# An edge-list graph kernel: GpSimd differences in the histogram, edge groups every 6.0 slots

## The chip, the cores and the metric

The kernel runs on one core of one Trainium2 chip. The metric is the device time of one execution in microseconds (us); lower is better. A profiled execution is traced instruction by instruction, and all rows below come from one such execution of the kernel before. Engines are named as in the profile: PE is TensorE's matmuls and PEld its weight loads, DVE is VectorE, ACT ScalarE, POOL GpSimd, SP SyncE, whose queue issues most plain transfers. A q behind a name (POOLq) is that engine's instruction queue.

## The reference

One graph layer over 6,250 nodes with 256 features and 200,000 edges (src, dst), sorted by dst:

```
out_deg = max(segment_sum(ones, src), 1);  in_cnt = segment_sum(ones, dst)
t1  = x @ W1
msg = (t1[src] + x[src] * x[dst] @ W2) / (sqrt(out_deg[src]) * sqrt(out_deg[dst]))
agg = segment_sum(msg, dst)
emb = leaky_relu(where(in_cnt > 0, t1 + agg, 0) + b, 0.01);  emb = emb / max(|emb|, 1e-12)
out = layernorm(x + emb)
```

Since the products with W1 and W2 are linear, the kernel sums scaled rows of x over the edges of a destination first, and multiplies by W1 and W2 once per block of 128 nodes.

## The kernel before

**Stage 1, the histogram of src.** It gives the out-degrees. A source number is split into a low part (7 bits) and a high part. The edges are cut into 98 groups of 16 tiles of 128 edges (`HT = 16`, one edge per partition and tile). For a group, VectorE makes the high hots (`hi_hot1`, L327: 16 x 50 columns, 1 where a ramp 0, 1, 2, ... equals the edge's high part) and, for a *plain* group, the low hots (`lo_hot1`, L336: 16 x 128 columns). Each of these is one tensor_tensor with is_equal, whose operands are the ramp (`iota_b`, in SBUF) and a pair-wise copy of the part (`hi2`, `lo2`). TensorE then does 16 matmuls of low by high hots, added up in `hist_ps` (L510).

For a *signed* group VectorE makes the high hots only. ScalarE makes steps in place of the low hots: 16 activations Sign of ramp + (0.5 - low), 128 columns each, with a bias per partition (`steps`, L445), which are -1 left of the edge's part and +1 from it on. They are added up in `step_ps` and turned into counts at the end by one matmul with a matrix of differences (`differ`, L536). Groups whose number modulo 11 is 3, 7 or 10 are signed: 26 of 98; 72 are plain.

Order and buffers: each engine goes through its own list of groups in order. VectorE may make the high hots of group g when group g - 4's matmuls are done (`HI_RING = 4`), the low hots of a plain group when those of the plain group two before are; the steps have two buffers as well. In between, VectorE does at group 8 the tables for the gathers (`gather_tables`) and at group 16 the keys of the edge lists (`list_keys`, L369 to L376); before groups 4 to 15 it waits for one gathered set of list rows each (`s_wrow`). TensorE turns the lists from group 17 on (`turn_lists`), and ScalarE copies them (`list_table`). GpSimd issues the 15 gathers of list rows, then four affine_selects (L273, L276), then waits for the end of the stage.

**Scaling.** With the degrees known, VectorE and ScalarE scale x and split it into three 16-bit parts (`yp`), and SP's queue stores them to `y_parts` in DRAM, in 8 chunks.

**Stage 2, the node blocks.** A loop over slots, written out by hand, gives every engine its order. 30 of the 49 node blocks are *dense*: their edges are counted into matrices (per slot, a window of 4 matmuls, L818, from hots that VectorE makes at L948 against a ramp in PSUM, `iota_w`) and multiplied with `yp` (L837, 9 or 12 matmuls per slot from slot 16 to 495). 19 blocks are *gathered*: 77 groups of 8 x 128 edges, whose rows GpSimd gathers from `y_parts` (L702, 8 indirect DMAs a group, 4 groups of buffers), and TensorE adds them up with hots (`group`, L799 and L805). VectorE adds a group's sums to `gT` and `cnt` three slots later (`accumulate`); TensorE's next group waits for that. Group g stands at slot `FIRST_SLOT + g * SLOTS_A_GROUP[0] // SLOTS_A_GROUP[1]`, 17 + 6.2 g, and is moved back where it would meet the sums of a gathered block. Each block has an end: its sums (gathered blocks: `turn_sums`, L853 and L854), transposes (`turn_uv`, L864), the weights (L876), then normalization on VectorE and ScalarE and the store of the block's output. The ends of dense blocks stand every 16 slots (the last at 496), those of gathered blocks halfway between where their last group is in (the last three at 472, 488 and 504).

At the start of the stage VectorE copies the ramp into PSUM, makes the first hots, and clears `gT`, `cnt` and sets `ones_f` (L1033 to L1035). GpSimd sets one column of ones (L707), then waits for the last store of `y_parts` and starts the gathers. After that a third stage, for graphs that do not fit these lists, is passed over.

Of the kernel before, what the change touches and what calls it, by code (L numbers as in the profile page):

```python
# [41 lines left out]
SLOTS_A_GROUP = (62, 10)  # L42
# [8 lines left out]
HI_RING = 4  # L51
SIGN_PERIOD = 11
SIGN_GROUPS = (3, 7, 10)
# [9 lines left out]
def build(nc, x, src, dst, w1, w2, bias, src_t, dst_t, starts, spans, out):  # L63
# [32 lines left out]
    with ctx:  # L96
# [9 lines left out]
        iota_h = sb("iota_h", [P, P], F16)  # L106
        w1_sb = sb("w1_sb", [P, H, D], F32)
# [24 lines left out]
        s_hist = sem("s_hist"); s_histall = sem("s_histall"); s_deg = sem("s_deg"); s_sqrt = sem("s_sqrt")  # L132
        s_hi = sem("s_hi"); s_r1 = sem("s_r1"); s_mid = sem("s_mid"); s_lo3 = sem("s_lo3")
# [8 lines left out]
        with ph1:  # L142
# [13 lines left out]
            lo_hot1 = sb1("lo_hot1", [P, 2, HT, P], BF16)  # L156
            hi_hot1 = sb1("hi_hot1", [P, HI_RING, HT, HI_COLS], BF16)
# [67 lines left out]
            kept_by = {b: next(i for i in range(2, len(signed)) if signed[i - 2] >= g) for g, b in turn_at.items()}  # L225

            with nc.Block() as block:  # L227
# [51 lines left out]

                @block.vector  # L280
                def _(dve):
# [31 lines left out]
                    nc.vector.tensor_copy(iota_b[:, :], iota_i[:, :])  # L313
# [6 lines left out]
                    def factor_hots(g):  # L320

                        part = sum(g * HT >= t1 for _, t1 in PAIR_PARTS)
                        dve.wait_ge(s_pairs1, 2 * (part + 1))
                        at = slice(g * HT, (g + 1) * HT)
                        if g >= HI_RING:
                            dve.wait_ge(s_hist, g - HI_RING + 1)
                        last = nc.vector.tensor_tensor(  # L327
                            hi_hot1[:, g % HI_RING, :, :].rearrange("p t (c two) -> p t c two", two=2),
                            iota_b[:, 0:HI_COLS].rearrange("p (c two) -> p c two", two=2).unsqueeze(1)
                            .to_broadcast([P, HT, HI_COLS // 2, 2]),  # L330
                            hi2[:, at, :].unsqueeze(2).to_broadcast([P, HT, HI_COLS // 2, 2]), ALU.is_equal)
                        if g in plain:
                            i = plain.index(g)
                            if i >= 2:
                                dve.wait_ge(s_hist, plain[i - 2] + 1)
                            last = nc.vector.tensor_tensor(  # L336
                                lo_hot1[:, i % 2, :, :].rearrange("p t (c two) -> p t c two", two=2),
                                iota_b[:, :].rearrange("p (c two) -> p c two", two=2).unsqueeze(1)
                                .to_broadcast([P, HT, P // 2, 2]),
                                lo2[:, at, :].unsqueeze(2).to_broadcast([P, HT, P // 2, 2]), ALU.is_equal)  # L340
                        last.then_inc(s_hot1, 1)
# [38 lines left out]
                    for g in range(HIST_GROUPS):  # L380
# [48 lines left out]
                def _(act):  # L429
# [11 lines left out]
                    def steps(i):  # L441
                        if i >= 2:
                            act.wait_ge(s_hist, signed[i - 2] + 1)
                        for t in range(HT):
                            last = nc.scalar.activation(lo_step[:, i % 2, t, :], iota_b[:, :], ACT.Sign,  # L445
                                                        bias=half_lo[:, signed[i] * HT + t:signed[i] * HT + t + 1])
                        last.then_inc(s_step, 1)
# [6 lines left out]
                    for i in range(len(signed)):  # L454
# [25 lines left out]
                def _(pe):  # L480
# [20 lines left out]
                    def histogram(g):  # L501
                        pe.wait_ge(s_hot1, g + 1)
                        if g in signed:
                            i = signed.index(g)
                            pe.wait_ge(s_step, i + 1)
                            into, low = step_ps, lo_step[:, i % 2, :, :]
# [34 lines left out]
        with ph2:  # L541
# [45 lines left out]
            iota_w = ps2("iota_w", [P, 512])  # L587
            iota_ps = iota_w[:, :].bitcast(F16)
# [4 lines left out]
            s_iotap = sem("s_iotap")  # L593
# [81 lines left out]
            with nc.Block() as block:  # L675
# [18 lines left out]
                def _(pool):  # L694
# [13 lines left out]
                    nc.gpsimd.drain().then_inc(s_ones, 1)  # L708
                    pool.wait_ge(s_ystore, 16 * len(X_CHUNKS))
# [73 lines left out]
                def _(pe):  # L783
# [116 lines left out]
                def _(dve):  # L900
# [164 lines left out]

        ph3 = ExitStack()
# [306 lines left out]
```

## Time and profile before

| | |
|---|---|
| median of 3 runs | 1077.23 us (1076.64 to 1593.53) |
| profiled execution | 1077.94 us, span of its instructions 1076.2 us |
| TensorE busy | 916.7 us (85%) in 13,011 matmuls |
| VectorE busy | 706.6 us (66%) |
| GpSimd busy | 610.5 us (57%), 586.8 of it the 616 gathers of L702 |
| ScalarE busy | 482.6 us (45%) |
| chain that ended last | TensorE 68%, VectorE 15%, issue 7%, GpSimd 6%, DMA 2% |

The shares are means over stages with different limits, so they are read together with the stretches of the stages: the histogram up to about 162 us, the scaling to 205, the start of the node blocks to about 223, the node blocks to about 1045 and their end. The chain of waits is followed back from the last instruction; what stands in it set the end at that place. In the groups of instructions, "idle before" is the idle time of the engine just before them, and behind the arrow stands what ended it.

### The profile page before, as it was taken

Reading aid. Unit: us, or ns where it says so; the run is one execution under the profiler, and the core shown is the slowest. Engines: PE = TensorE matmul, PEld = TensorE weight load, DVE = VectorE, ACT = ScalarE, POOL = GpSimd, SP = SyncE. Lnnn points to the kernel's source line nnn. Section 1 sums busy time; section 2 is a strip of 40 time slices with the busy share of each in tenths; the row PEclk is TensorE's granted clock in tenths of the full one; section 3 lists DMA queues with packets and bytes.
Section 4 is the critical chain, followed back from the end, with each engine's and each line's share of the span. In section 5 each row is a group of like instructions: output and inputs, shape, how many; then the busy total and the mean of one; then the engine's idle time right before and its main releaser. Section 6 shows DMA issues by size and latency. Waiting matters only on the chain.

```text
span 1076.2 us, 31326 instructions
## 1 busy us (share of the span) xinstructions
PE 916.7 (85%) x13011; PEld 813.4 (76%) x13011; DVE 706.6 (66%) x1524; ACT 482.6 (45%) x1357; POOL 610.5 (57%) x651
## 2 busy tenths in 40 slices
PE   3366660189999999999999999999999999999993
PEld 2255550078988888888988988988989888888882
DVE  8999998954566565665666566656656567466443
ACT  5799977343343343433434333433334334343311
POOL 4400000177777777777777775767767577777300
PEclk9985555589999999999999999999999999999995
DMA  9200003755566656566566655656646466566300
GB/s 314 67 2 2 2 2 135 253 158 161 168 170 177 179 168 179 167 177 178 170 172 176 175 167 144 177 148 176 178 145 178 136 177 180 157 173 170 94 20 21
DMA packets 68120, 155.83 MB, mean 145 GB/s; under 512 B 12006, under 2 KB 37668, under 8 KB 67972
## 3 DMA queue, kind: packets, MB, share of 16 engines
q0 software_dynamic: 40144, 123.12, 40.5%
q1 hardware_dynamic: 27828, 30.65, 8.7%
q8 instruction: 104, 1.70, 0.7%
q14 instruction: 44, 0.36, 0.1%
HBM read 137.69 MB, written 16.03 MB: 143 GB/s over the span
## 4 chain that ended last, share of the span: by engine, by line
PE 68%; DVE 15%; issue 7%; POOL 6%; DMA 2%; DVEq 1%; ACT 0%; POOLq 0%; ACTq 0%
PE g_ps L837 39%; PE grp_ps L799 8%; PE emb_ps L876 8%; PE win_ps L818 8%; POOL y_rows L702 6%; DVE hi_hot L327 4%; DVE lo_hot L336 3%; PE grp_ps L805 2%; DVE xs L420 2%; PE uvT_ps L864 2%; DVE yp L406 1%; DMA yp<-in_spans_dram,widx 1%; DVE yp L304 1%; PE hist_ps L510 1%; PE grp_ps L854 1%
## 5 line engine op out<-in xcount | busy, mean ns | idle before, releaser
L702 POOL DMA_INDIRECT y_rows<-y_parts,idx_tab x616 | 586.8, 953 | 214.3 <-issue 181.7
L837 PE MATMUL g_ps<-yp,counts 128*128 128x256 bf16 (+1 forms) x4410 | 566.5, 273 | 0.0
L837 PEld LDWEIGHTS g_ps<-yp,counts 128*128 128x128 f16 x4410 | 406.1, 98 | 47.6
L731 ACT CAST counts<-win_ps 128x392 f16<-128x392 f32 x480 | 231.1, 484 | 439.0 <-PE win_ps L818 433.8
L948 DVE TENSOR_TENSOR key_hot<-iota_w,pairs 128x1568 f16<-128x1568 f16 x120 | 116.4, 970 | 257.4 <-PE win_ps L818 256.0
L818 PE MATMUL win_ps<-key_hot,lo_hot 128*128 128x98 f16 x1920 | 167.2, 210 | 50.6 <-DVE lo_hot L948 49.6
L818 PEld LDWEIGHTS win_ps<-key_hot,lo_hot 128*128 128x128 f16 x1920 | 129.8, 99 | 71.7 <-DVE lo_hot L948 50.6
L948 DVE TENSOR_TENSOR lo_hot<-iota_w,pairs 128x2048 f16<-128x2048 f16 x120 | 146.6, 1222 | 46.9 <-PE win_ps L818 46.3
L445 ACT ACTIVATE yp<-iota_b,half_lo 128x128 bf16<-128x128 bf16 x416 | 122.3, 392 | 0.8 <-PE step_ps L510 0.8
L799 PEld LDWEIGHTS grp_ps<-hot,y_rows 128*128 128x128 bf16 x3696 | 103.8, 96 | 15.3 <-issue 10.3
L799 PE MATMUL grp_ps<-hot,y_rows 128*128 128x48 bf16 x3696 | 106.0, 183 | 9.7 <-DVE cnt L928 7.0
L510 PE MATMUL hist_ps<-hi_hot,lo_hot 128*128 128x50 bf16 x1152 | 58.8, 215 | 61.0 <-DVE lo_hot L336 61.0
L510 PEld LDWEIGHTS hist_ps<-hi_hot,lo_hot 128*128 128x128 bf16 x1152 | 49.9, 116 | 70.0 <-DVE lo_hot L336 69.8
L876 PE MATMUL emb_ps<-w_sb,uvT 128*128 128x256 f32 x392 | 96.5, 391 | 3.7 <-ACT uvT L749 3.7
L707 POOL MEMSET yp<- 128x98 bf16 x1 | 0.2, 184 | 163.9 <-POOLq L227 163.9
L336 DVE TENSOR_TENSOR lo_hot<-iota_b,lo 128x2048 bf16<-128x2048 bf16 x72 | 87.5, 1216 | 0.0
L876 PEld LDWEIGHTS emb_ps<-w_sb,uvT 128*128 128x128 f32 x392 | 72.8, 196 | 13.3 <-ACT uvT L749 4.3
L327 DVE TENSOR_TENSOR hi_hot<-iota_b,hi 128x800 bf16<-128x800 bf16 x98 | 53.7, 566 | 2.7 <-DMA yp<-in_spans_dram,widx 2.7
L755 ACT ACTIVATE ysum<-emb 128x256 f32<-128x256 f32 x49 | 20.5, 418 | 41.7 <-DVE emb L1002 40.1
L763 ACT ACTIVATE std<-veps 128x1 f32<-128x1 f32 x49 | 10.0, 203 | 57.6 <-DVE veps L1016 56.7
L1000 DVE SCALAR_TENSOR_TENSOR emb<-emb_ps,has,bias_sb 128x256 f32<-128x256 f32 x49 | 23.1, 472 | 17.7 <-PE emb_ps L876 17.7
L864 PE MATMUL uvT_ps<-ident,uv 128*128 128x128 f32 x196 | 29.9, 275 | 3.1 <-DVE uv L975 3.1
(127 smaller groups left out, 662.4 us busy)
## 6 DMA issues: line engine op xcount, KB each, us to landing
y_rows<-y_parts,idx_tab POOLq DMA_INDIRECT x616
y_parts<-yp SPq DMA_DIRECT2D x6, 1344.0 KB, 5.1
xs<-in_x_dram SPq DMA_DIRECT2D x1, 6144.0 KB
xb<-in_x_dram SPq DMA_DIRECT2D x48, 128.0 KB
out_dram<-o_sb SPq DMA_DIRECT2D x48, 128.0 KB
src_i<-in_src_t_dram SPq DMA_DIRECT2D x1, 784.0 KB, 4.6
y_parts<-yp SPq DMA_DIRECT2D x1, 768.0 KB, 4.4
y_parts<-yp SPq DMA_DIRECT2D x1, 576.0 KB, 5.6
```

Of the source, the lines that this page charges most:

```text
L327: last = nc.vector.tensor_tensor(hi_hot1[:, g % HI_RING, :, :].rearrange("p t (c two) -> p t c two", two=2), iota_b[:, 0:HI_COLS].rearrang ...
L336: last = nc.vector.tensor_tensor(lo_hot1[:, i % 2, :, :].rearrange("p t (c two) -> p t c two", two=2), iota_b[:, :].rearrange("p (c two) - ...
L445: last = nc.scalar.activation(lo_step[:, i % 2, t, :], iota_b[:, :], ACT.Sign, bias=half_lo[:, signed[i] * HT + t:signed[i] * HT + t + 1])
L510: last = nc.tensor.matmul(into[:, 0:HI_COLS], low[:, t, :], hi_hot1[:, g % HI_RING, t, :], start=False, stop=False)
L702: nc.gpsimd.indirect_dma_start(out=y_rows[:, g % RING, t, :], out_offset=None, in_=y_dram[:, :], in_offset=bass.IndirectOffsetOnAxis(ap=id ...
L731: nc.scalar.copy(counts[:, c % 2, :, i * WN:(i + 1) * WN], win_ps[:, i % 2, 0:KEYS].rearrange("p (d s) -> p s d", s=BLOCKS)).then_inc(s_cn ...
L799: nc.tensor.matmul(grp_ps[:, at + h * W:at + (h + 1) * W], y_rows[:, g % RING, t, of:of + P], hot[:, g % 2, t, :], start=(t == 0 and m == ...
L818: last = nc.tensor.matmul(win_ps[:, i % 2, t * LKEYS:(t + 1) * LKEYS], lo_hot[:, (i // WQ) % 2, of, :], key_hot[:, (i // WQ) % 2, of, :], ...
L837: last = nc.tensor.matmul(g_ps[:, c % 2, 0:n], counts[:, c % 2, s, :], yp_1[:, s, m * D:m * D + n], start=(s == 0 and m == PARTS - 1), sto ...
L864: last = nc.tensor.transpose(uvT_ps[:, (i * H + h) * P:(i * H + h + 1) * P], uv[:, i, h * P:(h + 1) * P], ident[:, :])
L876: last = nc.tensor.matmul(emb_ps[:, 0:D], uvT[:, i * H + h, :], w[:, h, :], start=(i == 0 and h == 0), stop=(i == 1 and h == H - 1))
L948: last = nc.vector.tensor_tensor(hots[:, Q % 2, :, :].rearrange("p t (c two) -> p t c two", two=2), iota_ps[:, 0:cols].rearrange("p (c two ...
```

## The change

- A third kind of histogram group, *pooled*. The kinds are now given by a string of turns: the first 22 groups as before (V plain, S signed), then a period of 17 groups with 10 plain, 3 signed and 4 pooled (G). For a pooled group GpSimd makes the differences ramp + 0.5 - low for all 16 x 128 columns in one tensor_tensor (`lo_hotp`, two buffers), ScalarE takes their Sign in place in one activation, and TensorE adds them into `step_ps`. There are 61 plain, 19 signed and 18 pooled groups.
- VectorE's hots of the histogram read the ramp from PSUM (`iota_bps`); the PSUM bank is held from the first stage on, and the copy into it moves to the first stage. `HI_RING` is 6 in place of 4, and the waits for list rows before groups 4 to 15 are dropped (`list_keys` still waits for all of them).
- Groups of gathered rows stand at 17 + 6.0 g. The last group is at slot 478 in place of 494, the last three ends of gathered blocks at 456, 472 and 488 in place of 472, 488 and 504; the slot lists have 8 gaps of three slots in place of 13.
- GpSimd clears `gT` and `cnt` and sets `ones_f`, between its column of ones and its wait for the stores of `y_parts`.

```diff
-SLOTS_A_GROUP = (62, 10)
+SLOTS_A_GROUP = (60, 10)
-HI_RING = 4
-SIGN_PERIOD = 11
-SIGN_GROUPS = (3, 7, 10)
+HI_RING = 6
+FIRST_TURNS = 'VVVSVVVSVVS' * 2
+LATER_TURNS = 'VSVGVVGVSVVGVSVGV'
...
+        iota_w = numbers.enter_context(nc.psum_tensor("iota_w", [P, 512], F32))
+        iota_ps = iota_w[:, 0:P // 2].bitcast(F16)
+        iota_bps = iota_w[:, P // 2:P].bitcast(BF16)
...
+            turns = (FIRST_TURNS + LATER_TURNS * HIST_GROUPS)[:HIST_GROUPS]
+            signed, pooled, plain = ([g for g in range(HIST_GROUPS) if turns[g] == of] for of in 'SGV')
+            stepped = sorted(signed + pooled)
...
+                    pool.wait_ge(s_iotab, 1)
+                    for i, g in enumerate(pooled):
+                        pool.wait_ge(s_pairs1, 2 * (sum(g * HT >= t1 for _, t1 in PAIR_PARTS) + 1))
+                        if i >= 2:
+                            pool.wait_ge(s_hist, pooled[i - 2] + 1)
+                        nc.gpsimd.tensor_tensor(
+                            lo_hotp[:, i % 2, :, :].rearrange("p t (c two) -> p t c two", two=2),
+                            iota_half[:, :].rearrange("p (c two) -> p c two", two=2).unsqueeze(1)
+                            .to_broadcast([P, HT, P // 2, 2]),
+                            lo2[:, g * HT:(g + 1) * HT, :].unsqueeze(2).to_broadcast([P, HT, P // 2, 2]), ALU.subtract
+                        ).then_inc(s_lowp, 1)
...
-                    nc.vector.tensor_copy(iota_b[:, :], iota_i[:, :])
+                    nc.vector.tensor_scalar(iota_half[:, :], iota_i[:, :], 0.5, None, ALU.add)
+                    nc.vector.tensor_copy(iota_b[:, :], iota_i[:, :]).then_inc(s_iotab, 1)
+                    dve.wait_ge(s_iotab, 1)
+                    nc.vector.tensor_copy(iota_w[:, 0:P // 2], iota_h[:, :].bitcast(F32))
+                    nc.vector.tensor_copy(iota_w[:, P // 2:P], iota_b[:, :].bitcast(F32)).then_inc(s_iotap, 1)
+                    dve.wait_ge(s_iotap, 1)
...
-                            iota_b[:, 0:HI_COLS].rearrange("p (c two) -> p c two", two=2).unsqueeze(1)
+                            iota_bps[:, 0:HI_COLS].rearrange("p (c two) -> p c two", two=2).unsqueeze(1)
...
-                        if 4 <= g < KEYS_AT and g - 3 <= SETS:
-                            dve.wait_ge(s_wrow[g - 4], 16)
...
+                        if g in pooled:
+                            k = pooled.index(g)
+                            act.wait_ge(s_lowp, k + 1)
+                            low = lo_hotp[:, k % 2, :, :].rearrange("p t n -> p (t n)")
+                            last = nc.scalar.activation(low, low, ACT.Sign)
...
+                    nc.gpsimd.memset(cnt[:, :, :], 0.0)
+                    nc.gpsimd.memset(ones_f[:, :], 1.0)
+                    nc.gpsimd.memset(gT[:, :, :], 0.0)
+                    nc.gpsimd.drain().then_inc(s_zero, 1)
                     pool.wait_ge(s_ystore, 16 * len(X_CHUNKS))
...
-                    nc.vector.tensor_copy(iota_w[:, 0:P // 2], iota_h[:, :].bitcast(F32)).then_inc(s_iotap, 1)
-                    dve.wait_ge(s_iotap, 1)
                     place_hots(0, 0)
                     place_hots(0, 1)
-                    nc.vector.memset(gT[:, :, :], 0.0).then_inc(s_zero, 1)
-                    nc.vector.memset(cnt[:, :, :], 0.0).then_inc(s_zero, 1)
-                    nc.vector.memset(ones_f[:, :], 1.0).then_inc(s_zero, 1)
```

## Rows read from the trace of the kernel before

**Rows 1.** by stretch: busy PE, PEld, DVE, ACT, POOL; clock, DMA, GB/s

```profile
54.00:162.00 108.00, 66.36 (x1327) 58.46 (x1328) 107.92 (x142) 98.95 (x334) 0.00 (x0) 0.59 0.01 2
...
223.00:1045.00 822.00, 811.17 (x11195) 724.20 (x11194) 484.70 (x1187) 307.77 (x844) 577.34 (x606) 1.00 0.57 162
```

**Rows 2.** timeline of VectorE in the histogram: start us, us, engine, line, operation

```profile
154.88 0.56 DVE L327 TENSOR_TENSOR hi_hot<-iota_b,hi 128x800 bf16<-128x800 bf16 x1
...
155.37 1.21 DVE L336 TENSOR_TENSOR lo_hot<-iota_b,lo 128x2048 bf16<-128x2048 bf16 x1
...
156.50 0.56 DVE L327 TENSOR_TENSOR hi_hot<-iota_b,hi 128x800 bf16<-128x800 bf16 x1
```

**Rows 3.** groups of instructions: busy, mean ns of one, idle before

```profile
L445 ACT ACTIVATE yp<-iota_b,half_lo 128x128 bf16<-128x128 bf16 x416 | 122.3, 392 | 0.8 <-PE step_ps L510 0.8
...
L327 DVE TENSOR_TENSOR hi_hot<-iota_b,hi 128x800 bf16<-128x800 bf16 x98 | 53.7, 566 | 2.7 <-DMA yp<-in_spans_dram,widx 2.7
```

**Rows 4.** groups by shape: ScalarE's long activations in the first stage

```profile
L433 ACT CAST hi<-yp 128x2496 bf16<-128x2496 int32 x1 | 2.3, 2272 | 0.1
...
L436 ACT ACTIVATE half_lo<-yp 128x1568 f32<-128x1568 int32 x1 | 1.5, 1504 | 0.0
```

**Rows 5.** groups by shape: GpSimd's operations in the first stage

```profile
L276 POOL TENSOR_SCALAR_AFFINE_SELECT yp<-yp 128x128 f32<-128x128 f32 x3 | 2.1, 713 | 0.3
...
L259 POOL MEMSET xs<- 128x256 f32 x1 | 0.4, 405 | 0.2 <-issue 0.2
...
L261 POOL MEMSET ones_b<- 128x1 bf16 x1 | 0.1, 96 | 0.0
```

**Rows 6.** groups of instructions: VectorE's low hots in the node blocks

```profile
L948 DVE TENSOR_TENSOR lo_hot<-iota_w,pairs 128x2048 f16<-128x2048 f16 x120 | 146.6, 1222 | 46.9 <-PE win_ps L818 46.3
```

**Rows 7.** timeline of VectorE and GpSimd together, and of the list keys

```profile
37.16 1.31 DVE L336 TENSOR_TENSOR lo_hot<-iota_b,lo 128x2048 bf16<-128x2048 bf16 x1
...
37.59 1.03 POOL L273 TENSOR_SCALAR_AFFINE_SELECT ident<-ident 128x128 f32<-128x128 f32 x1
...
46.82 2.25 DVE L371 TENSOR_TENSOR yp<-yp,thr 128x1920 f32<-128x1920 int32 x1
```

**Rows 8.** timeline of TensorE at group 3; in brackets idle before and its releaser

```profile
24.65 0.82 PE L510 MATMUL step_ps<-hi_hot,yp 128*128 128x50 bf16 x16 [4.56 <-ACT yp L445]
```

**Rows 9.** timeline at the start of the node blocks

```profile
207.82 1.93 DVE L1033 MEMSET gT<- 128x2240 f32 x1 [0.42 <-issue]
...
210.47 0.95 POOL L702 DMA_INDIRECT y_rows<-y_parts,idx_tab  x1 [5.35 <-DMA y_parts<-yp]
```

**Rows 10.** timeline at group 8 of the gathered rows

```profile
299.26 0.95 POOL L702 DMA_INDIRECT y_rows<-y_parts,idx_tab  x1 [0.30 <-issue]
...
303.23 1.38 PE L799 MATMUL grp_ps<-hot,y_rows 128*128 128x48 bf16 x48 [1.18 <-DMA y_rows<-y_parts,idx_tab]
```

**Rows 11.** timeline of TensorE's slots and ends; two slots from second row to third

```profile
309.57 0.60 PE L864 MATMUL uvT_ps<-ident,uv 128*128 128x128 f32 x4
...
310.00 0.34 PE L818 MATMUL win_ps<-key_hot,lo_hot 128*128 128x98 f16 x4
...
312.37 1.89 PE L876 MATMUL emb_ps<-w_sb,uvT 128*128 128x256 f32 x8
...
314.10 0.34 PE L818 MATMUL win_ps<-key_hot,lo_hot 128*128 128x98 f16 x4
...
316.46 0.38 PE L853 MATMUL grp_ps<-ident,gb 128*128 128x128 f32 x2
...
317.08 0.35 PE L818 MATMUL win_ps<-key_hot,lo_hot 128*128 128x98 f16 x4
```

**Rows 12.** waits: engine, line, waited for: us in total, times, longest

```profile
PE grp_ps L799 <- DVE cnt L928: 7.0, 13, 0.6
```

**Rows 13.** timeline of the last two outputs on VectorE

```profile
1059.70 0.41 DVE L1026 TENSOR_SCALAR o_sb<-ysum,mv,rstd 128x256 f32<-128x256 f32 x1
...
1067.85 0.41 DVE L1026 TENSOR_SCALAR o_sb<-ysum,mv,rstd 128x256 f32<-128x256 f32 x1
```

More of the change, by code:

```diff
@@ L106, in build @@
         iota_h = sb("iota_h", [P, P], F16)
+        numbers = ExitStack()
+        iota_w = numbers.enter_context(nc.psum_tensor("iota_w", [P, 512], F32))
+        iota_ps = iota_w[:, 0:P // 2].bitcast(F16)
+        iota_bps = iota_w[:, P // 2:P].bitcast(BF16)
         w1_sb = sb("w1_sb", [P, H, D], F32)
@@ L132, in build @@
         s_hist = sem("s_hist"); s_histall = sem("s_histall"); s_deg = sem("s_deg"); s_sqrt = sem("s_sqrt")
+        s_iotab = sem("s_iotab"); s_iotap = sem("s_iotap"); s_lowp = sem("s_lowp")
         s_hi = sem("s_hi"); s_r1 = sem("s_r1"); s_mid = sem("s_mid"); s_lo3 = sem("s_lo3")
@@ L156, in build @@
             lo_hot1 = sb1("lo_hot1", [P, 2, HT, P], BF16)
+            lo_hotp = sb1("lo_hotp", [P, 2, HT, P], BF16)
+            iota_half = sb1("iota_half", [P, P], BF16)
             hi_hot1 = sb1("hi_hot1", [P, HI_RING, HT, HI_COLS], BF16)
@@ L216, in build @@
             wt_ps = ps1("wt_ps", [P, 2, 512])
-            signed = [g for g in range(HIST_GROUPS) if g % SIGN_PERIOD in SIGN_GROUPS]
-            plain = [g for g in range(HIST_GROUPS) if g not in signed]
+            turns = (FIRST_TURNS + LATER_TURNS * HIST_GROUPS)[:HIST_GROUPS]
+            signed, pooled, plain = ([g for g in range(HIST_GROUPS) if turns[g] == of] for of in 'SGV')
+            stepped = sorted(signed + pooled)
             list_batches = [(k, s, min(4, SETS - s)) for s in range(0, SETS, 4) for k in range(2)]
             turn_at = {KEYS_AT + 1 + TURN_STEP * b: b for b in range(len(list_batches))}
-            kept_by = {b: next(i for i in range(2, len(signed)) if signed[i - 2] >= g) for g, b in turn_at.items()}
+            kept_by = {b: next(i for i in range(2, len(stepped)) if stepped[i - 2] >= g) for g, b in turn_at.items()}
             with nc.Block() as block:
@@ L337, in factor_hots @@
                                 lo_hot1[:, i % 2, :, :].rearrange("p t (c two) -> p t c two", two=2),
-                                iota_b[:, :].rearrange("p (c two) -> p c two", two=2).unsqueeze(1)
+                                iota_bps[:, :].rearrange("p (c two) -> p c two", two=2).unsqueeze(1)
                                 .to_broadcast([P, HT, P // 2, 2]),
@@ L441, in steps @@
                     def steps(i):
[L442 to L446, printed above, removed]
+                        g = stepped[i]
+                        if g in pooled:
[3 more added lines that the diff above has]
+                            last = nc.scalar.activation(low, low, ACT.Sign)
+                        else:
+                            k = signed.index(g)
+                            if k >= 2:
+                                act.wait_ge(s_hist, signed[k - 2] + 1)
+                            for t in range(HT):
+                                last = nc.scalar.activation(lo_step[:, k % 2, t, :], iota_b[:, :], ACT.Sign,
+                                                            bias=half_lo[:, g * HT + t:g * HT + t + 1])
                         last.then_inc(s_step, 1)
@@ L452, in list_table @@
                         nc.scalar.copy(tab[:, k, s * P:(s + m) * P], wt_ps[:, b % 2, 0:m * P]).then_inc(s_wtc, 1)
-                    for i in range(len(signed)):
+                    for i in range(len(stepped)):
                         if i == kept_by[0] - 1:
@@ L502, in histogram @@
                         pe.wait_ge(s_hot1, g + 1)
[L503 to L506, printed above, removed]
+                        if g in stepped:
+                            pe.wait_ge(s_step, stepped.index(g) + 1)
+                            into, low = step_ps, (lo_hotp[:, pooled.index(g) % 2, :, :] if g in pooled
+                                                  else lo_step[:, signed.index(g) % 2, :, :])
                         else:
@@ L846, in turn_sums @@
                         if b == 0:
-                            pe.wait_ge(s_zero, 3)
+                            pe.wait_ge(s_zero, 1)
                         pe.wait_ge(s_gb, 2 * b + 2)
@@ L915, in accumulate @@
                         if g == 0:
-                            dve.wait_ge(s_zero, 3)
+                            dve.wait_ge(s_zero, 1)
                         base = nc.vector.value_load(base_i[0:1, g:g + 1], min_val=0, max_val=NEAR * P)
@@ L1060, in _ @@
                             layer_norm(n)
+        numbers.close()
         ph3 = ExitStack()
```

3 lines of the change are left out of this document (removed).

## The prediction

> **What bounds the kernel now.** I read the busy time by stretch first. From 54 to 162 us, where the histogram groups 16 to 97 run, VectorE is busy for 107.92 of 108.00 us, ScalarE for 98.95, GpSimd for nothing, TensorE for 66.36 at a granted clock of 0.59. From 223 to 1045 us TensorE is busy for 811.17 of 822 us at full clock [rows 1]. So the change works on two stages with different limits: VectorE in the histogram, TensorE in the node-block stage; the scaling between them is not touched. The profiled execution took 1077.94 us, 0.71 above the median of 1077.23; the sum is made against 1077.94 and the forecast is put beside the median.
>
> **Histogram: what VectorE gets rid of.** A plain group costs VectorE a high and a low hot. Their starts follow at 0.49 and 1.13 us [rows 2], so a plain group holds it for 1.62 us and any other for 0.49 (the high hot alone). Counting the turn string: 61 plain groups (72 before), 19 with ScalarE's signs alone (26), 18 with GpSimd's differences; the first 22 groups are as before. 11 low hots at 1.13 us are 12.4 us less on VectorE. That is the upper bound of the gain here.
>
> **What ScalarE gets.** A group of its own is 16 activations, 122.3 us / 416 x 16 = 4.70 us [rows 3]. For a pooled group it does one Sign over 2,048 columns in place. No such row exists; the long forms took 1.504 us for 1,568 columns and 2.272 for 2,496 [rows 4], 0.83 ns per column, so 2,048 take 1.90; back to back some 0.1 of an activation overlaps (392 ns in length, 294 apart [rows 3]), so 1.81 to 1.90; I take 1.85. Now 17 later groups (3 S, 4 G, 10 V) need: VectorE 17 x 0.49 + 10 x 1.13 = 19.6 us; ScalarE 3 x 4.70 + 4 x 1.85 = 21.5 us. ScalarE is late next, not VectorE. Before, 11 groups cost VectorE 11 x 0.49 + 8 x 1.13 = 14.4 us: 1.31 us a group against 21.5 / 17 = 1.265. Over the 76 later groups: 76 x 0.045 = 3.4 us. With 1.81 or 1.90 for the Sign it is 4.1 or 2.6. ScalarE has some slack before group 22 that the rings of two can carry over, so I take **3.8 us** of the 12.4.
>
> **What GpSimd gets.** 4 differences per 17 groups; below 21.5 / 4 = 5.4 us each they hide beside ScalarE, above it GpSimd sets the pace. No row shows a two-input operation on GpSimd. The nearest: a memset of 256 columns took 0.405 us and of one column 0.096 [rows 5], 1.2 ns per column, which makes 2.6 us for 2,048 (it reads nothing: the low end); a select over 128 columns, which reads and writes, took 0.713 [rows 5], and if all of it grows with the columns that makes 11.4 us (the high end). Ends this far apart straddle 5.4. The select must have a fixed part as the memsets have, and a subtraction does less per column than an index compare with a fill, so I stand nearer the memset, at 4 to 5 us: hidden. Each microsecond above 5.4 costs 16 (two of the 18 differences can be made ahead, the ring of two holds the rest).
> The Trainium skill's GPSIMD Engine Reference, "Performance versus the Vector engine", gives 4.5 us for a float32 two-input operation of 2,048 columns; by that price nothing in the sum changes.
>
> **Ramp number in PSUM.** VectorE's hots now read it there. In the second stage it already does: 128x2048 of 16-bit type took 1.222 us from PSUM [rows 6] against 1.21 from SBUF [rows 2]. Cost 0.
> The Trainium skill, "VectorE: DVE Perf Modes", "The perf-mode tier table", says the opposite: with any PSUM operand tensor_tensor falls to one element a cycle; row and rule differ, and the row decides, with a small chance left (rivals).
>
> **Neighbours on the SBUF port.** While GpSimd's select of 1.03 us ran, a low hot took 1.31 instead of 1.21 us [rows 2, 7]; both its inputs were in SBUF. Later hots have one. But GpSimd's first two differences follow its selects (37.59 + 1.03 + 3 x 0.71 = 40.8 us [rows 5, 7]) and lie beside the list keys, one of which has two SBUF inputs (46.82, 2.25 us [rows 7]); by that row it costs 0.1 us, at worst the rest of a difference, 3 us (a rival).
>
> **Dropped waits on the list rows.** VectorE idled 2.7 us on one [rows 3]. Nothing comes of it: the low hot of group 6 needs group 4's matmuls, which stand behind group 3's signs; TensorE began those at 24.65, after 4.56 us of waiting for ScalarE [rows 8]. The three extra VectorE instructions at the start (about 0.7 us by the hots' fixed part) vanish in the same wait.
>
> **Node blocks: the start.** The three memsets leave VectorE (gT alone 1.93 us [rows 9]), so windows 4 to 16 come earlier. That gives 0: the first gather starts at 210.47, when the y_parts stores land [rows 9], and the gathers pace the first groups: 8 a group; the 72nd, the last of group 8, was issued at 299.26 [rows 10], so one per 88.79 / 71 = 1.25 us and 10.0 us a group; its matmuls began at 303.23 after 1.18 us of waiting [rows 10]. On GpSimd the memsets lie before the store wait, in which it idled 5.35 us; 2,240 + 1,120 columns at 1.2 ns are 4.1 us. Cost 0; if they take twice that, 3 us.
>
> **6.0 slots.** TensorE's work stays the same, it only moves against the end and the gathers. A slot takes 1.185 us, the transpose of an end 0.43, its weights 1.73, the transposes of gathered sums 0.62 [rows 11].
> - At the front: group 9 moves from slot 78 to 71. Its rows land at 210.47 + 79 x 1.25 + 3.97 = 313.2. TensorE used to pass that point at 303.23 + some 1.6 (group 8: 1.38 for its 48 matmuls [rows 10], and 8 more) + 5 x 1.185 + 0.43 = 311.2. It waits: **+2.0**. From group 10 on 6 slots with ends need over 10.0 us, and the gathers get ahead.
> - Groups three slots apart: TensorE waited 13 times, 7.0 us, for the addition of the group before [rows 12]. By the slot lists there are 8 such gaps instead of 13: **-2.7**.
> - At the end: the ends stood at 488, 496 (dense), 504 (gathered). Now the gathered one is at 488 and the dense at 496 the last. The outputs of the last two were written at 1059.70 and 1067.85 [rows 13]: the second falls away, **-8.15**; its 0.62 + 0.43 + 1.73 on TensorE move into the full stretch, **+2.8**.
> Together -6.0.
>
> **Sum**: -3.8 - 6.0 = -9.8, 1068.1 for the profiled execution, 1067.4 against the median, 0.9% less. About 2% is what a measurement of this kernel tells from no change, so this counts as within.
>
> **Rivals.**
> 1. *GpSimd sets the pace* (slower). For it: the high end [rows 5]. Against it: that end gives the select no fixed part. With T for one difference: group 25 is done near 54 + 10 x 1.31 = 67 us, then 16 differences run end to end, the histogram ends at 67 + 16 T + 3.5 us (the last Sign, two groups' matmuls), against 162 before [rows 1]. At T = 5.7 the histogram gains nothing, at 6.1 the whole change is lost, at 7 it ends at 182.5, so 1077.2 + 20.5 - 6.0 = 1092, at 7.5 over 2% (1100), at 11.4 1162. Chance 0.19, of which 0.10 above 7.5.
> 2. *One part fails to come.* Only the tail: 1071 (ScalarE waits for GpSimd's pairs, or the list keys lose 3 us to the first differences, which holds up the Signs behind them). Only the histogram: 1073 (gathers late for more groups than one; the spare is little: 10.0 us against 822 / 77 x 6.0 / 6.2 = 10.3 [rows 1]). Chance 0.17.
> The Trainium skill, "SBUF — State Buffer", "Who interferes with whom", holds that whichever of the two starts first has the port for its whole instruction, which is the 3 us; the 0.1 us [rows 7] speaks against it for a short one.
> 3. *PSUM halves VectorE's rate.* A column costs 0.52 ns by the two hots (1.21 us for 2,048, 0.56 for 800); one more 0.52 on 61 x 2,048 and 98 x 800 columns is 106 us, less the 12.4 and 6.0 from above: 1165. [rows 6] speaks against it. Chance 0.02. It is the rule cited above from the Trainium skill's "VectorE: DVE Perf Modes".
> 4. *More than forecast*: ScalarE's Sign overlaps better and VectorE's 12.4 us come in full: 1059. The 21.5 us against 19.6 speak against it. Chance 0.05, with 0.02 past 2%.
>
> **Numbers.** Forecast 0.57. Range 1062 to 1082: rival 2, the bounds of the Sign, of the memsets and of rival 1 up to T = 6.5; 0.05 lies below, some 0.15 above. Faster by over 2%: 0.02; slower by over 2%: 0.12 (rival 1 above 7.5 and rival 3); within: 0.86.
>
> **What would show it.** Differences on GpSimd under 5.4 us; ScalarE busy without gaps from 60 to 156 us and TensorE waiting for its Signs, with gaps of VectorE between the hots; hots at 1.22 us; the histogram's last matmul near 158; first gather as long after the stores as before; a wait for rows at group 9; one output after the last product. GpSimd back to back with ScalarE idle would make it wrong, as would hots of 2.3 us, or waits for rows past group 12.

## The result: 2.55 us faster where 9.8 were forecast

The kernel after the change takes 1074.37 us (median of 14 runs, 1073.67 to 1074.87) against 1076.92 before: a ratio of 0.9977, with a 95% interval of 0.997 to 0.9985. One of the 14 runs before took 1593.53 us; the ratio is made from runs without such a disturbance. The time after lies inside the range (1062 to 1082) and on the forecast's side, but only a quarter of the forecast gain came. The profiled execution went from 1077.94 to 1074.59 us, its span from 1076.2 to 1072.8. Four marks in the two traces cut this into stages.

| mark | before | after | change |
|---|---|---|---|
| histogram: last matmul of the steps (`zeros_b`) starts | 162.66 | 157.78 | -4.88 |
| first gather starts | 210.47 | 205.56 | -4.91 |
| last product matmul ends | 1045.41 | 1048.19 | +2.78 |
| last output starts | 1067.85 | 1062.38 | -5.47 |
| end of the span | 1076.2 | 1072.8 | -3.40 |

The histogram gave 4.9 us. The stretch of the products grew from 834.94 us to 842.63, a loss of 7.7. What comes after the products shrank by 8.25, and what comes after the last output grew by 2.07. The sum: -4.91 + 7.69 - 8.25 + 2.07 = -3.40.

**Histogram after.** By stretch, in the columns of [rows 1]:

```profile
54.00:162.00 108.00, 61.07 (x1345) 56.27 (x1345) 98.83 (x141) 101.61 (x247) 57.56 (x16) 0.68 0.01 2
...
223.00:1045.00 822.00, 807.70 (x11106) 719.78 (x11105) 489.43 (x1197) 309.69 (x848) 573.88 (x602) 1.00 0.57 161
```

Against [rows 1] VectorE is no longer full (98.83 of 108 us, and this stretch now holds the first 4 us after the histogram), ScalarE stands at 101.61 us in place of 98.95, and GpSimd's 57.56 us stand where nothing was. The end of ScalarE's steps, before and then after (its last steps, then its next instruction):

```profile
139.70 15.86 ACT L445 ACTIVATE yp<-iota_b,half_lo 128x128 bf16<-128x128 bf16 x54
162.91 0.20 ACT L463 COPY step_sums<-step_ps 128x49 f32<-128x49 f32 x1 [7.35 <-PE step_ps L531]
```

```profile
151.99 3.73 ACT L472 ACTIVATE lo_hotp<-lo_hotp 128x2048 bf16<-128x2048 bf16 x2
158.00 0.20 ACT L496 COPY step_sums<-step_ps 128x49 f32<-128x49 f32 x1 [2.28 <-PE step_ps L564]
```

ScalarE is done at 155.56 us before and at 155.72 after, no earlier; what shrank is the time it then waits for the other engines, from 7.35 to 2.28 us.

The groups of instructions (busy, mean ns of one | idle time before):

```profile
L296 POOL TENSOR_TENSOR lo_hotp<-iota_half,lo 128x2048 bf16<-128x2048 bf16 x18 | 64.7, 3608 | 51.4 <-PE step_ps L543 51.3
...
L364 DVE TENSOR_TENSOR lo_hot<-iota_w,lo 128x2048 bf16<-128x2048 bf16 x61 | 74.3, 1217 | 8.7 <-PE hist_ps L543 8.6
...
L355 DVE TENSOR_TENSOR hi_hot<-iota_w,hi 128x800 bf16<-128x800 bf16 x98 | 52.4, 565 | 0.0
```

A difference takes 3.608 us, a high hot 565 ns and a low hot from PSUM 1.217 us, as against [rows 2, 3]. The timeline shows who sets the pace:

```profile
81.77 0.82 PE L543 MATMUL step_ps<-hi_hot,yp 128*128 128x50 bf16 x16 [3.55 <-ACT yp L478]
...
81.86 1.93 ACT L472 ACTIVATE lo_hotp<-lo_hotp 128x2048 bf16<-128x2048 bf16 x1
...
83.30 1.23 DVE L364 TENSOR_TENSOR lo_hot<-iota_w,lo 128x2048 bf16<-128x2048 bf16 x1 [1.42 <-PE hist_ps L543]
...
83.68 3.04 ACT L478 ACTIVATE yp<-iota_b,half_lo 128x128 bf16<-128x128 bf16 x10
...
84.91 3.61 POOL L296 TENSOR_TENSOR lo_hotp<-iota_half,lo 128x2048 bf16<-128x2048 bf16 x1 [3.61 <-PE step_ps L543]
```

ScalarE's Sign of 2,048 columns starts at 81.86 and its next activations 1.82 us later. TensorE waited 3.55 us for ScalarE's steps. VectorE, which may fill a buffer of low hots again only when TensorE is done with it, then waited 1.42 us before a low hot. The waits from 55 to 165 us add it up (total, times, longest):

```profile
PE step_ps L543 <- ACT yp L478: 30.3, 11, 3.6
...
PE step_ps L543 <- ACT lo_hotp L472: 3.9, 10, 0.8
...
DVE lo_hot L364 <- PE hist_ps L543: 6.5, 11, 1.4
```

**Node blocks after.** TensorE's waits from 223 to 1045 us, the answer to [rows 12]:

```profile
PE grp_ps L887 <- DVE cnt L962: 6.1, 9, 0.7
...
PE grp_ps L833 <- DVE cnt L962: 4.6, 8, 0.9
...
PE grp_ps L833 <- DMA y_rows<-y_parts,idx_tab: 3.6, 5, 1.1
```

The waits at the groups of gathered rows (L833, L799 before) fell from 13 to 8. But L887 is new to this list: that is the transpose of a gathered block's sums (`turn_sums`, L853 before), and it waits 9 times, 0.68 us each. Before it waited once:

```profile
PE grp_ps L853 <- DVE cnt L928: 0.7, 1, 0.7
...
PE grp_ps L799 <- DMA y_rows<-y_parts,idx_tab: 2.7, 3, 1.2
```

One such stall, on TensorE and on VectorE:

```profile
315.81 0.41 PE L887 MATMUL grp_ps<-ident,gb 128*128 128x128 f32 x2 [0.68 <-DVE cnt L962]
...
316.65 1.16 PE L871 MATMUL g_ps<-yp,counts 128*128 128x256 bf16 x9
...
314.18 1.22 DVE L982 TENSOR_TENSOR lo_hot<-iota_w,pairs 128x2048 f16<-128x2048 f16 x1 [0.20 <-PE win_ps L852]
...
315.32 0.24 DVE L960 TENSOR_TENSOR gT<-gT,grp_ps 128x96 f32 x1
...
315.48 0.19 DVE L962 TENSOR_TENSOR cnt<-cnt,grp_ps 1x48 f32 x1
```

The last group's addition (L960 and L962) ran to 315.67, right behind a low hot; the transpose of the sums could start at 315.81 only, and the products of the next slot behind it.

The gathers start when the stores of `y_parts` have landed, as in [rows 9], with 2.22 us of waiting left of the 5.35:

```profile
205.56 0.97 POOL L732 DMA_INDIRECT y_rows<-y_parts,idx_tab  x1 [2.22 <-DMA y_parts<-yp]
```

**The end.** The last output on VectorE after the change ([rows 13] before), then SyncE's wait for the last stores, after and before:

```profile
1062.38 0.41 DVE L1060 TENSOR_SCALAR o_sb<-ysum,mv,rstd 128x256 f32<-128x256 f32 x1
```

```profile
SPq L705 <- DMA out_dram<-o_sb: 3.7, 1, 3.7
```

```profile
SPq L675 <- DMA out_dram<-o_sb: 1.3, 1, 1.3
```

One output is left after the last product, but the store behind it took 2.4 us longer to land. The last block is now block 48, which has 106 rows and not 128.

### The profile page after: what moved, and what is told of

Its sections match the earlier page's. It is cut to its first block, busy times and chain, and to the rows that moved or that the text cites. A ratio compares the mean times of both kernels' runs of the same rounds, so it can differ in the third digit from the quotient of the medians.

```text
span 1072.8 us, 31264 instructions
## 1 busy us (share of the span) xinstructions
PE 910.1 (85%) x13011; PEld 809.1 (75%) x13011; DVE 695.2 (65%) x1512; ACT 483.8 (45%) x1263; POOL 673.0 (63%) x672
## 4 chain that ended last, share of the span: by engine, by line
PE 69%; ACT 10%; DVE 9%; POOL 6%; issue 4%; DMA 1%; DVEq 1%; POOLq 0%
PE g_ps L871 39%; PE grp_ps L833 8%; PE emb_ps L910 8%; PE win_ps L852 8%; ACT yp L478 6%; POOL y_rows L732 6%; ACT lo_hotp L472 3%; PE grp_ps L839 2%; PE uvT_ps L898 2%; DVE xs L445 2%; DVE yp L431 1%; DVE yp L327 1%; DMA y_rows<-y_parts,idx_tab 1%; DVE lo_hot L364 1%; PE grp_ps L887 1%
## 5 line engine op out<-in xcount | busy, mean ns | idle before, releaser
L833 PEld LDWEIGHTS grp_ps<-hot,y_rows 128*128 128x128 bf16 x3696 | 104.1, 96 | 15.5 <-DMA y_rows<-y_parts,idx_tab 7.5
L833 PE MATMUL grp_ps<-hot,y_rows 128*128 128x48 bf16 x3696 | 106.4, 183 | 9.9 <-DMA y_rows<-y_parts,idx_tab 5.3
L296 POOL TENSOR_TENSOR lo_hotp<-iota_half,lo 128x2048 bf16<-128x2048 bf16 x18 | 64.7, 3608 | 51.4 <-PE step_ps L543 51.3
L478 ACT ACTIVATE yp<-iota_b,half_lo 128x128 bf16<-128x128 bf16 x304 | 90.6, 405 | 0.8 <-PE step_ps L543 0.8
L364 DVE TENSOR_TENSOR lo_hot<-iota_w,lo 128x2048 bf16<-128x2048 bf16 x61 | 74.3, 1217 | 8.7 <-PE hist_ps L543 8.6
L543 PE MATMUL hist_ps<-hi_hot,lo_hot 128*128 128x50 bf16 x976 | 46.3, 212 | 27.8 <-DVE lo_hot L364 27.8
L543 PEld LDWEIGHTS hist_ps<-hi_hot,lo_hot 128*128 128x128 bf16 x976 | 41.1, 115 | 31.3 <-DVE lo_hot L364 30.6
L355 DVE TENSOR_TENSOR hi_hot<-iota_w,hi 128x800 bf16<-128x800 bf16 x98 | 52.4, 565 | 0.0
L543 PE MATMUL step_ps<-hi_hot,yp 128*128 128x50 bf16 x304 | 14.7, 210 | 38.1 <-ACT yp L478 35.3
L543 PEld LDWEIGHTS step_ps<-hi_hot,yp 128*128 128x128 bf16 x304 | 12.9, 114 | 39.5 <-issue 33.3
```

The costliest lines, as they stand in the source:

```text
L296: nc.gpsimd.tensor_tensor(lo_hotp[:, i % 2, :, :].rearrange("p t (c two) -> p t c two", two=2), iota_half[:, :].rearrange("p (c two) -> p ...
L355: last = nc.vector.tensor_tensor(hi_hot1[:, g % HI_RING, :, :].rearrange("p t (c two) -> p t c two", two=2), iota_bps[:, 0:HI_COLS].rearra ...
L364: last = nc.vector.tensor_tensor(lo_hot1[:, i % 2, :, :].rearrange("p t (c two) -> p t c two", two=2), iota_bps[:, :].rearrange("p (c two) ...
L478: last = nc.scalar.activation(lo_step[:, k % 2, t, :], iota_b[:, :], ACT.Sign, bias=half_lo[:, g * HT + t:g * HT + t + 1])
L543: last = nc.tensor.matmul(into[:, 0:HI_COLS], low[:, t, :], hi_hot1[:, g % HI_RING, t, :], start=False, stop=False)
L833: nc.tensor.matmul(grp_ps[:, at + h * W:at + (h + 1) * W], y_rows[:, g % RING, t, of:of + P], hot[:, g % 2, t, :], start=(t == 0 and m == ...
```

## The experiments

The expectations set a theory A against rivals. A follows from what the traces above show: ScalarE paces the histogram, the slots of 6.0 put a group one slot ahead of the sums of 9 blocks, and the last block's 106 rows are slow to store. "After" below is the changed kernel; the ratios are against the kernel before.

**1. After with groups every 6.2 slots.** Does the histogram alone give the whole gain?

```diff
-SLOTS_A_GROUP = (60, 10)
+SLOTS_A_GROUP = (62, 10)
```

> The whole change but for the group spacing, which is 6.2 slots again. Theory A (the histogram gave its 4.9 us, and the 6.0 slots took some 1.5 back: +7.7 before the end of the products, of it 6.1 us of waits of the sums' transposes for the addition of a group one slot ahead, -8.3 after it, +2.1 for a slower last store): 1076.9 - 4.9 = 1072.0, 2.4 us faster than the changed kernel. Theory B (the spacing gave its 6 us and something else in the change took them): about 1080. In the trace A wants the last product near 1040.5, one such wait instead of nine and the last store in 16 parts again.

Measured 1073.3 us, ratio 0.996 (0.9946 to 0.9974). That is 1.3 us above A's 1072.0, of which about half is the kernel before itself (1077.45 beside this run, 1076.9 in A's sum).

```profile
PE grp_ps L833 <- DVE cnt L962: 7.7, 13, 0.9
PE grp_ps L887 <- DVE cnt L962: 0.7, 1, 0.7
...
SPq L705 <- DMA out_dram<-o_sb: 1.3, 1, 1.3
```

With 6.2 slots the sums wait once, the groups 13 times and the last store 1.3 us, as in the kernel before. The stretch of the products is 835.87 us against 834.94. So all but some 0.9 us of its growth belongs to the 6.0 slots, and the rest of the change by itself is worth 4.2 us (1077.45 to 1073.3), near the 3.8 that the histogram was to give.

**2. Before with groups every 6.0 slots.** The same step by itself.

```diff
-SLOTS_A_GROUP = (62, 10)
+SLOTS_A_GROUP = (60, 10)
```

> The kernel before with groups every 6.0 slots and nothing else. Theory A: 1076.9 + 7.7 - 8.3 + 2.1 = 1078.4, slower than before by 1.5 us, with nine waits of 0.7 us before the transposes of the sums. Theory B: 1071, faster by 6.

Measured 1079.01 us, ratio 1.0013 (1.0004 to 1.0022).

```profile
PE grp_ps L853 <- DVE cnt L928: 6.2, 9, 0.7
PE grp_ps L799 <- DMA y_rows<-y_parts,idx_tab: 4.7, 6, 1.4
PE grp_ps L799 <- DVE cnt L928: 4.5, 8, 0.7
...
SPq L675 <- DMA out_dram<-o_sb: 3.7, 1, 3.7
```

The step for which the prediction wrote -6.0 makes the kernel slower by 1.6 us. The nine waits and the slow store come with it and need nothing else of the change.

**3. After with the last store cut in 96 and 10 rows.**

```diff
-                        sp.dma_start(out[at:at + m, :], o_sb[0:m, :]).then_inc(s_out[n % 2], 16)
+                        cut = m // 16 * 16 if n == len(ends) - 1 else m
+                        sp.dma_start(out[at:at + cut, :], o_sb[0:cut, :]).then_inc(s_out[n % 2], 16)
+                        if cut < m:
+                            sp.dma_start(out[at + cut:at + m, :], o_sb[cut:m, :]).then_inc(s_out[n % 2], 16)
...
```

> The changed kernel with the last output store, 106 rows, cut into 96 rows and 10. Theory A (106 rows go over two DMA engines, as the two semaphore packets of that store show against 16 of a 128-row store, and with the change this store is the last): the time after the last output falls from 10.0 to about 8 us, 1072.3. Theory B (the end is longer for another reason, the last barrier or code loading): 1074.4, no change.

Measured 1072.44 us, ratio 0.9951 (0.9938 to 0.9965); the span ends 8.35 us after the last output starts (1062.15 to 1070.5), where it was 10.42 in after.

```profile
SPq L705 <- DMA out_dram<-o_sb: 1.0, 1, 1.0
```

The wait falls from 3.7 to 1.0 us and the span by 2.3. The extra 2.07 us at the end were the store's.

**4. After with the groups kept clear of the sums.** Gaps of four slots at least, and no group of a later block in the slot before a block's sums; 5.95 slots a group make up for the room.

```diff
-SLOTS_A_GROUP = (60, 10)
+SLOTS_A_GROUP = (595, 100)
...
-                    if at <= slots[g] < at + SUMS_AFTER + 2:
+                    if at - 1 <= slots[g] < at + SUMS_AFTER + 2 and g > last_group(b + LAG):
...
-                        slots[g] = max(slots[g], slots[g - 1] + 3)
+                        slots[g] = max(slots[g], slots[g - 1] + 4)
```

> The changed kernel with groups every 5.95 slots, none in the slot ahead of a gathered block's sums, and none less than four slots behind another. Theory A (TensorE's waits for additions, 9 x 0.7 before the transposes and 8 x 0.6 before groups, are lost time in a full stage): 10.7 us of waits go, some 1 us more waiting for gathered rows comes at the front: about 1065. Theory B (the gathers at 10.0 us a group set the stage's length, and the waits are spare time that comes back as waits for rows): 1073 to 1074.

Measured 1065.02 us, ratio 0.9885 (0.987 to 0.99): 9.35 us less than after. All of TensorE's waits of 223 to 1045 us:

```profile
PE grp_ps L833 <- DMA y_rows<-y_parts,idx_tab: 5.2, 6, 1.2
PE uvT_ps L898 <- DVE uv L1009: 2.0, 1, 2.0
PE emb_ps L910 <- ACT uvT L783: 1.9, 4, 0.5
```

Both kinds of waits for additions are gone, 10.7 us in all; in the stretch of the products waits for rows and for ScalarE's `uvT` took 3.5 more (the 2.0 for `uv` lies behind it). That stretch is 833.53 us, 9.1 less. That is more than the 7.2 of the waits: TensorE's busy time fell by 1.84 us as well (823.69 to 821.85) for the same work. 17 stalls are gone and 5 came (one for rows, four for `uvT`), so a stall costs some 0.1 to 0.15 us beside its wait, by an estimate from these counts.

**5. After with all three mended**: the last store cut, the groups apart, and other turns with fewer activations for ScalarE.

```diff
-LATER_TURNS = 'VSVGVVGVSVVGVSVGV'
+LATER_TURNS = 'VVGVSVVGGVVVVSG'
...
```

> The changed kernel with the groups apart (5.95 slots, none one slot ahead of the sums, none under four behind another), the last store cut in two, and the later turns V V G V S V V G G V V V V S G (15 groups: 9 plain, 2 signed, 4 pooled). Theory A, the three gains add: 1065.0 - 2.0 - 7.0 = 1056. Theory B, the turns gain nothing because two pooled groups in a row find the ring of two full: 1063.

Measured 1056.21 us, ratio 0.981 (0.9797 to 0.9824). Alone, 3, 4 and 7 (below) have spans 2.3, 9.6 and 6.8 us shorter than after, together 18.7; here it is 17.3 (1072.8 to 1055.5). So they are three separate limits, which nearly add up.

**6. After with the hots' ramp read from SBUF.** What did moving it to PSUM bring?

```diff
-                            iota_bps[:, :].rearrange("p (c two) -> p c two", two=2).unsqueeze(1)
+                            iota_b[:, :].rearrange("p (c two) -> p c two", two=2).unsqueeze(1)
...
```

> The changed kernel with the histogram's ramp read from SBUF again, so that VectorE's hots have two SBUF inputs while GpSimd makes differences. Theory A (the two engines exclude each other for whole instructions): 17 groups need 19.6 us of VectorE plus 4 x 3.6 us of GpSimd = 34 us in place of 21.5, the histogram 76 / 17 x 12.5 = 56 us longer, 1130. Theory B (0.1 us for each hot that meets a difference, as one hot beside a select before): some 5 hots for each of 18 differences, 9 us on VectorE, most of it in its slack of 1.9 us per 17 groups: 1074 to 1076.

Measured 1130.17 us, ratio 1.0497 (1.0481 to 1.0513). The groups of instructions from 55 to 200 us:

```profile
L296 POOL TENSOR_TENSOR lo_hotp<-iota_half,lo 128x2048 bf16<-128x2048 bf16 x15 | 107.9, 7211 | 45.5 <-PE step_ps L543 45.5
...
L364 DVE TENSOR_TENSOR lo_hot<-iota_b,lo 128x2048 bf16<-128x2048 bf16 x47 | 70.6, 1501 | 21.2 <-PE hist_ps L543 21.2
...
L355 DVE TENSOR_TENSOR hi_hot<-iota_b,hi 128x800 bf16<-128x800 bf16 x79 | 55.7, 737 | 0.0
...
L472 ACT ACTIVATE lo_hotp<-lo_hotp 128x2048 bf16<-128x2048 bf16 x16 | 30.4, 1905 | 37.9 <-POOL lo_hotp L296 37.9
```

With both inputs of VectorE's hots in SBUF the means are 7.211 us for a difference in place of 3.608, 1.501 for a low hot in place of 1.217 and 0.737 for a high hot in place of 0.565, and ScalarE idles 37.9 us for differences. The means hide what happens: over the whole run a low hot takes 1.209 to 4.600 us (median 1.218), a high hot 0.559 to 3.974 (median 0.562) and a difference 3.602 to 16.496 (median 3.951).

```profile
122.93 16.50 POOL L296 TENSOR_TENSOR lo_hotp<-iota_half,lo 128x2048 bf16<-128x2048 bf16 x1 [5.39 <-PE step_ps L543]
...
126.33 1.21 DVE L364 TENSOR_TENSOR lo_hot<-iota_b,lo 128x2048 bf16<-128x2048 bf16 x1
...
143.04 4.60 DVE L364 TENSOR_TENSOR lo_hot<-iota_b,lo 128x2048 bf16<-128x2048 bf16 x1 [7.08 <-PE hist_ps L543]
...
156.50 16.49 POOL L296 TENSOR_TENSOR lo_hotp<-iota_half,lo 128x2048 bf16<-128x2048 bf16 x1 [5.39 <-PE step_ps L543]
```

The difference that starts at 122.93 lasts until 139.43. VectorE's hots beside it keep their 1.21 us, and VectorE has to stop for TensorE at 135.96 (143.04 less its wait of 7.08): the difference ends 3.5 us later, which is about what it takes alone. The low hot at 143.04 starts while a later difference runs and takes 4.60 us. So the two engines held each other back for whole instructions, and hots that follow without a gap held a difference for as long as they lasted. That is theory A, in the time and in the rows: four differences serve 17 groups, and the next four start at 156.50, 33.57 us later, where A has 34.

In effect this is the prediction's rival 1, the histogram late for GpSimd. Its formula 67 + 16 T + 3.5 gives 186 us for a mean T of 7.2, and the last matmul of the steps started even later, at 213.52: the differences were not made end to end as the formula has it, GpSimd also waited 45.5 us for TensorE.

The Trainium skill, "SBUF — State Buffer", "Who interferes with whom", says that a VectorE instruction with two SBUF inputs contends with a GpSimd instruction that reads SBUF, and that one with at most one SBUF input, outside VectorE's 2-port modes, does not. This run and the profile after agree: up to 16.496 us for a difference here, 3.604 to 3.610 for all 18 there.

**7. After with the other turns alone**, the diff of 5 without the rest.

> The changed kernel with the later turns V V G V S V V G G V V V V S G and nothing else. Theory A (ScalarE paces the histogram of the changed kernel): 15 groups need 2 x 4.70 + 4 x 1.82 = 16.7 us of ScalarE, 15 x 0.485 + 9 x 1.135 = 17.5 of VectorE and 14.4 of GpSimd, 1.17 us a group in place of 1.265: 76 x 0.1 = 7 us less, 1067.4, with ScalarE waiting now and then. Theory B (GpSimd with its ring of two is near its limit too, and pooled groups in a row wait): 1072 to 1078.

Measured 1067.75 us, ratio 0.9919 (0.9904 to 0.9934). Of the shorter stretch from 54 to 150 us, first after, then this kernel:

```profile
54.00:150.00 96.00, 55.54 (x1230) 51.19 (x1230) 90.05 (x124) 93.41 (x234) 55.39 (x16) 0.68 0.01 2
```

```profile
54.00:150.00 96.00, 62.25 (x1326) 55.03 (x1326) 96.00 (x133) 89.11 (x196) 64.61 (x18) 0.65 0.01 2
```

With 2 signed and 4 pooled of 15 groups ScalarE has room (89.11 of 96 us), VectorE is full again, and the last matmul of the steps starts at 151.26 in place of 157.78. Over the whole histogram there are 16 signed, 20 pooled and 62 plain groups in place of 19, 18 and 61. That takes 3 x 4.70 - 2 x 1.82 = 10.5 us off ScalarE. So ScalarE was what limited the histogram after the change.

**8. After with the three memsets back on VectorE.**

```diff
-                    nc.gpsimd.memset(gT[:, :, :], 0.0)
...
+                    nc.vector.memset(gT[:, :, :], 0.0).then_inc(s_zero, 1)
...
```

> The changed kernel with the three memsets on VectorE again. Theory A (the gathers, which start when the y_parts stores land, pace the first groups): no change, 1074.4, with windows 5 to 16 3 us later and a shorter wait for rows at group 0. Theory B (the memsets were on the path): 1077.5.

Measured 1073.93 us, ratio 0.9972 (0.9962 to 0.9981), no different from after.

```profile
205.35 0.97 POOL L732 DMA_INDIRECT y_rows<-y_parts,idx_tab  x1 [5.34 <-DMA y_parts<-yp]
```

The first gather starts where it did (205.56 after): the stores of `y_parts` set it, and the memsets only fill 3.1 us of the wait.

**9. Kernel 5 with GpSimd's differences held back until the list keys are done.**

```diff
                     pool.wait_ge(s_iotab, 1)
+                    pool.wait_ge(s_wkey, 1)
```

> The kernel with the groups apart, the cut store and the other turns, and GpSimd's first difference held back until VectorE's list keys are done. Theory A (the list key that took 4.0 in place of 2.5 us stood behind GpSimd's second difference): it takes 2.4 to 2.5 us, the keys end 1.5 us earlier and all behind them, 1056.2 - 1.5 = 1054.7. Theory B (the 1.5 us are hidden, or the first differences now come late for group 24): 1056 or more.

Measured 1054.78 us, ratio 0.9799 (0.9785 to 0.9812), the lowest time here. GpSimd's first two differences after the change and the key that meets the second of them, then the same key in this kernel:

```profile
36.17 7.17 POOL L296 TENSOR_TENSOR lo_hotp<-iota_half,lo 128x2048 bf16<-128x2048 bf16 x2
...
41.45 4.02 DVE L397 TENSOR_SCALAR yp<-yp 128x1920 int32<-128x1920 int32 x1
```

```profile
41.49 2.52 DVE L398 TENSOR_SCALAR yp<-yp 128x1920 int32<-128x1920 int32 x1
```

Alone the key takes 2.52 us. After the change it starts at 41.45, beside a difference that runs until 43.34 and loses nothing (7.17 us for the two), and takes 4.02. The histogram's last matmul starts at 149.63 against 151.21 in kernel 5. The times of the two kernels have intervals that overlap, so the 1.4 us between them rest on the trace.

## Why the prediction was wrong

**The step that failed is "6.0 slots"**, put at "together -6.0". With what hangs on it, it came out at about +1.5 (7.69 - 8.25 + 2.07), and at +1.6 in experiment 2, where it is the only change. Its three points, as the prediction has them:

- *Front, +2.0 for rows at group 9.* Group 9 waited 1.00 us for its rows; all waits for rows from 223 us on went from 2.7 to 3.6 us, +0.9 (to 4.7, +2.0, in experiment 2).
- *Groups three slots apart, -2.7.* The 13 waits became 8, and 7.0 us became 4.6: -2.4.
- *End, -8.15, and its work +2.8.* From the last product to the last output: 22.44 us before, 14.19 after, -8.25. The moved work is in the count of matmuls before the last product's end: 11,269 with 6.0 slots, 11,253 with 6.2 (experiment 1), 16 more, which is one gathered end (2 + 2 + 4 + 8).

None of these three explains the miss. The step put two other things at nothing, without a reason. The first is the waits of the sums: the slot lists were searched for gaps between groups only. The sums of a block wait for the addition of the group before them just as the next group does, and before the change one block in 19 had a group one slot ahead of its sums. At 6.0 the two periods lock: four groups take 24 slots, the ends of gathered blocks stand 16 and 32 slots apart by turns, the group before the sums stands 1 or 5 slots ahead by turns, and 9 of 19 stand at one. That is 6.1 - 0.7 = +5.4 us of waiting. The second is the last store: the last block to be stored changed from one of 128 rows to one of 106, +2.07, shown by experiment 3.

The stretch of the products adds up so: +5.4 - 2.4 + 0.9 + 2.8, and +0.4 at its start (the 21st window's matmuls stand 30.17 us after the first gather against 29.75), make 7.1 of the 7.7; the stalls' own 0.1 us, and small waits that shifted, were not separated further.

The other steps held, the list keys apart:

- **Histogram, -3.8: measured -4.9**, with the mechanism as forecast: ScalarE late next, TensorE waiting for it, gaps of VectorE. Of the bounds the Sign's pitch of 1.81 was the near one (1.82 measured), which makes 4.1 by the prediction's figures. The sum compares paces per group and misses a plainer limit: ScalarE's work did not shrink. It had 26 x 4.70 = 122.2 us of steps before and has 19 x 4.70 + 18 x 1.82 = 122.1 after, and was done at 155.56 and 155.72. The gain is the tail behind that: the last matmul of the steps started 7.10 us after it before and 2.06 after.
- **GpSimd's difference, 4 to 5 us: 3.608**, nearer the memset than I stood. The high end was not only too far, its row was a poor one: the same selects [rows 5] took 295 and 304 ns after the change, with no VectorE instruction of two SBUF inputs beside them. Experiment 6, with the ramp back in SBUF, brings 715 and 1,022 back (713 and 1,027 before): the row was mostly waiting.
- **Hots from PSUM, cost 0**: 1.217 us against the 1.21 of [rows 2]. The Trainium skill's "VectorE: DVE Perf Modes", "The perf-mode tier table", which would have made it about double, does not hold for these 16-bit hots. What the ramp in PSUM saves was in no part of the sum: rival 1 lost because of it, and experiment 6 puts a price on it, 56 us. The prediction says only that later hots have one input in SBUF, so that the differences stayed hidden was in part luck.
- **List keys, 0.1 us, 3 at worst**: 1.5 us, at L397 (L369 before) and not at the key with two inputs, which [rows 7] had been read for. The 0.1 us was read beside a select that takes 0.3 us alone; the key waited for what was left of a difference, as the 3 us of rival 2 had it (experiment 9).
- **Dropped waits on list rows and memsets, 0**: VectorE waits 2.18 us at the low hot of group 6 instead, and experiment 8 shows the memsets.

Experiment 5 shows that about 20 us were to be had from the same parts: the change was held back by the order of the slots, the split of the turns and the last store.

## What to carry to other kernels

When a period in a schedule written by hand is changed, list the distance from every producer to every consumer of its result, not only the one that the change aims at; here the periods 6 and 16 repeated one bad distance in 9 of 19 blocks. When the last item of a loop changes, look at its shape: what is hidden for all the others is bare at the end. Before an engine is relieved of work, add up what the next one has to do in all: ScalarE's 122 us stayed as they were. Before work is given to GpSimd beside VectorE, see that VectorE's tensor_tensors there have at most one input in SBUF, and time the rest: the key of experiment 9 has one input and was held all the same.

## What the runs showed of the hardware

- VectorE's tensor_tensor with two SBUF inputs and GpSimd's held each other back for whole instructions (experiment 6): a low hot took 1.21 or up to 4.60 us, a high hot 0.56 or up to 3.97, and a difference up to 16.50 us, as it was held until VectorE's hots left a gap. With one input in PSUM a difference took 3.61 us and the hots 1.22 and 0.57. A tensor_scalar of 1,920 int32 columns on VectorE beside a difference took 4.02 us in place of 2.52.
- GpSimd's gathers of the list rows were slowed too: in the mean of 15, 966 ns after the change and 1,235 in experiment 6, where the ramp's place is the only difference (1,203 before).
- A store of 106 rows took longer than one of 128: 3.7 us of waiting against 1.3. In the transfers of the last store's stretch the packets under 512 bytes tell the two apart: 2 for 106 rows, 16 for 128, and 26 for 96 + 10 (16 + 10). The three lines are of after, of before and of experiment 3:

```profile
DMA packets 114, 0.17 MB, mean 15 GB/s; under 512 B 2, under 2 KB 108, under 8 KB 108
```

```profile
DMA packets 151, 0.20 MB, mean 25 GB/s; under 512 B 16, under 2 KB 144, under 8 KB 144
```

```profile
DMA packets 138, 0.17 MB, mean 20 GB/s; under 512 B 26, under 2 KB 132, under 8 KB 132
```

The Trainium skill, "DMA: Bandwidth & Descriptors", "Why a DMA increments its semaphore by 16 and not by 1", says that a transfer uses as many engines, up to 16, as divide the rows, which is 2 for 106 and 10 for 10; the 2, 16 and 26 packets agree. It gives no time for it; the 2.4 us are measured here.
